# Scores times values on half the rows of the array: two 64-token products with a PSUM bank each, in place of one 128-token product

## The chip, the cores and the metric

The kernel runs on one core of one Trainium2 chip. The metric is the device time of one execution in microseconds (us); the time before is the median of three runs. The engines are named as in the profile: PE is TensorE's matrix multiplication, PEld its loading of the stationary operand, DVE the vector engine, ACT the scalar engine, POOL GpSimd, SP the engine that issues most of the DMAs.

## What is computed

Two layers over one sequence of 4096 tokens of width 256, all in fp32. Each layer normalizes the tokens (`xn`), and adds to the stream an attention-like part and a mixture of experts. The change is in the first layer's attention-like part:

```python
CHUNK = 32
Q = x @ W_q.T
K = x @ W_k.T
V = x @ W_v.T
decay = jax.nn.sigmoid(log_decay[0])
pos = jnp.arange(C)                      # C = CHUNK
diff = pos[:, None] - pos[None, :]
mask = jnp.where(diff >= 0, decay ** diff, 0)
...
S = jnp.einsum('bncd,bnkd->bnck', Qc, Kc) * mask
O = jnp.einsum('bnck,bnkd->bncd', S, Vc).reshape(B, T, D)
gate = jax.nn.sigmoid(x @ W_g.T)
out = gate * O @ W_o.T + x
```

A token sees only the tokens of its own chunk of 32, up to itself. Seen over 128 tokens the score matrix is therefore block-diagonal, in blocks of 32, and so also in blocks of 64. The first layer's other part has 16 experts (keys 256x128, values 128x256 each), all of which run for every token. The second layer is a linear scan with four mixtures and eight routed experts; the change does not touch it.

## The kernel before

The first layer runs over eight groups of 512 tokens (`GROUPS` = 8, `GT` = 512), a group being `JT` = 4 tiles of 128 tokens; the width 256 is `DC` = 2 parts of 128. Within a group a loop `for k in range(E0)` goes over the 16 experts. For expert k PE runs `up(k + 1)`, six matmuls with 512 moving columns into PSUM bank 0 or 1 (helper `mm3`, L397 to L399), and then `down(k)`, twelve matmuls with 256 moving columns into banks 2 to 5 (L1218 to L1220). ACT makes the rounded half of the hidden tile (`relu_hi`, L896), DVE the remainder (`relu_lo`, L1015), and `down(k)` waits for that remainder. Both engines also take the results of `down` out of PSUM (DVE L1060, ACT L936).

The attention-like part is slipped in between experts, in a fixed order written out by hand. It shares banks 6 and 7 (`side2 = ps[:, 6:8, :]`), whose use is passed on through the semaphores `side_full` (PE has written) and `side_free` (ACT or DVE has read).

- After `down(4)` PE makes the scores (L1281): for each tile, each of the two parts of the width and each half h of 64 tokens, one matmul with all 128 rows of the array and 64 of its columns. Half 0 uses columns 0 to 63 of the array, half 1 columns 64 to 127. The halves alternate. DVE masks them into `s32` (L1081), only the two 64x64 diagonal blocks of each tile; the rest of `s32` was set to zero once (`trim_mask`).
- After `down(7)` PE multiplies scores and values (L1289): for each part c of the width and each tile j one fp32 matmul, 128 tokens on 128 rows, 128 columns stationary (`v32`), 128 columns moving (`s32`). Each fp32 matmul shows in the trace as two matmul records with a load each, so eight matmuls show as sixteen. The last one signals `side_full`.
- DVE then multiplies the result with the gate into `sig_g` (L1093, one instruction over 128x1024) and signals `o_gate`; two transposes (L1097) stand behind it in DVE's order. ACT waits for `o_gate` and makes `oT_h` (L954), and only then `relu_hi` of expert 9; DVE's `relu_lo(9)` follows that, and PE's `down(9)` waits for it.
- DVE makes `oT_l` (L1101) behind that. PE needs both after `down(11)` for the output projection (L1236 to L1238).

All engines run the groups from the same `body(g, first, last)`: group 0, a hardware loop over groups 1 to 5, and groups 6 and 7, so that the product occurs 8 times in an execution. The second layer starts when the first has ended on PE. The lines on which matmuls of both layers lie (L397 to L399) are those of a helper.

Of the kernel before, what the change touches and what calls it, by code (L numbers as in the profile page):

```python
# [27 lines left out]
ALU = mybir.AluOpType  # L28
# [3 lines left out]
P = 128  # L32
# [4 lines left out]
JT = GT // P  # L37
# [12 lines left out]
N_ROUND = (NSLOT + 1) // ROUND  # L50
CHUNK = 32
Q32 = 32
S64 = 64
NL = M + E1
VS = D + E0
# [9 lines left out]
def build(nc, a, out):  # L65
# [13 lines left out]
    def sem(name):  # L79
        return nc.alloc_semaphore(name)  # L80
# [44 lines left out]
    sig_g = ra("sig_g", [P, DC, GT], F32)  # L125
    v32 = ra("v32", [P, JT, D], F32)
    s32 = ra("s32", [P, JT, P], F32)
# [5 lines left out]
    otmp = sig_g[:, 0, :].rearrange("p (j d) -> p j d", j=2)  # L133
    N_Q = P // Q32
    xq = v32[:].rearrange("p j (h k) -> p (j h) k", k=DC * Q32)
    stats0 = ra("stats0", [P, JT, 6], F32)
# [12 lines left out]
    at_post = ra.at  # L149
    gw = ra("gw", [P, DC, P // Q32, Q32], F32R)  # L150
    gw_raw = ra("gw_raw", [P, DC, Q32], F32)
    lgT = ra("lgT", [P, JT, Q32], F32)
    lg_rows = ra("lg_rows", [P, JT, Q32], F32)
    stats1 = ra("stats1", [P, JT, 6], F32)
# [96 lines left out]
    ps = nc.alloc_psum_tensor("ps", [P, 8, 512], F32)  # L251
    side2 = ps[:, 6:8, :]
# [95 lines left out]
    o_gate, o_hi, o_23 = sem("o_gate"), sem("o_hi"), sem("o_23")  # L348
# [23 lines left out]
    def use(g, name, first=False):  # L372

        start = 2 if first else 8 * g + 1
        return start + USES.index(name)
# [92 lines left out]
    def chunk_of(rows, j, c):  # L468

        return rows[:, j, c:D:DC]  # L470
# [71 lines left out]
    def mixture_transpose(pe, mx, part, bank):  # L542
        pe.wait_ge(r_comb, part)
        return pe.transpose(ps[0:mixture_rows(mx), bank, 0:P], mx["comb"][:].rearrange("p t m -> p (t m)"), ident[:])
# [155 lines left out]
    with nc.Block("all") as block:  # L700
# [285 lines left out]
        def _(dve):  # L986
# [47 lines left out]
            def body(g, first, last):  # L1034
# [12 lines left out]
                for k in range(E0):  # L1047
# [27 lines left out]
                    if k == 4:  # L1075
# [3 lines left out]
                        for h, done in ((0, mask_s_near), (1, side_free)):  # L1079
                            t = slice(h * S64, (h + 1) * S64)  # L1080
                            dve.tensor_tensor(s32[t, :, t], ps[t, 6, 0:JT * S64].rearrange("p (j c) -> p j c", j=JT),  # L1081
                                              maskT[t, t].unsqueeze(1).to_broadcast((S64, JT, S64)),
                                              ALU.mult).then_inc(done, 1)
                    if k in (10, 11) and not first:
                        c = k - 10
# [4 lines left out]
                        gate_logits(dve, g - 1)  # L1090
                    if k == 7:
                        dve.wait_ge(side_full, use(g, "o", first) + 1)
                        dve.tensor_tensor(sig_g[:], side2, sig_g[:], ALU.mult).then_inc(o_gate, 1)  # L1093
                    if k == 7 and not first:
                        dve.wait_ge(nq_in, 16 * N_Q * g)
                        for c in range(DC):
# [1 line left out]
                    if k in (8, 9):  # L1098
                        c = k - 8
# [30 lines left out]
                    if k == 5 and first:  # L1130
                        dve.wait_ge(gw_ready, 1)
                        gate = gw_raw[:, :, 0:NL].unsqueeze(2).to_broadcast((P, DC, P // Q32, NL))
# [24 lines left out]
            with dve.Fori(1, GROUPS - 2) as g:  # L1157
                body(g, False, False)
            body(GROUPS - 2, False, False)
            body(GROUPS - 1, False, True)  # L1160

        @block.tensor
        def _(pe):
            def body(g, first, last):
                def ready(name):
                    pe.wait_ge(side_free, freed(g, name, first))

                def weights(name):
                    if first:
                        pe.wait_ge(w_lo, chunks[name][0] + 1)  # L1170

                def up(k):

                    if first and k == 0:
                        pe.wait_ge(k0_lo, 1)
                    else:
                        weights(f"keys{k // 4}")
                    if not (first and k < 2):
                        pe.wait_ge(h_lo, E0 * g + k - 1)
                    s = slice(k * H0, (k + 1) * H0)  # L1180
                    for c in range(DC):
                        if k == 0:
                            if first:
                                pe.wait_ge(side_hi, 1 + c)
                            else:
                                pe.wait_ge(xT_hi_ok, DC * (g - 1) + c + 1)
                            pe.matmul(ps[:, 0, :], keys_h[:, c, s], xT_h[:, c, :], start=c == 0, stop=False)
                            pe.matmul(ps[:, 0, :], keys_l[:, c, s], xT_h[:, c, :], start=False, stop=False)
                            continue
                        last = mm3(pe, ps[:, k % 2, :], keys_h[:, c, s], keys_l[:, c, s], xT_h[:, c, :], xT_l[:, c, :],  # L1190
                                   c == 0, c == DC - 1)
                    if k == 0:
                        for c in range(DC):
                            if first:
                                pe.wait_ge(side_free, 1 + c)
                            else:
                                pe.wait_ge(xT_lo_ok, DC * (g - 1) + c + 1)
                            last = pe.matmul(ps[:, 0, :], keys_h[:, c, s], xT_l[:, c, :], start=False, stop=c == DC - 1)
                    last.then_inc(h_full, 1)
# [23 lines left out]
                def project(n):  # L1223
                    weights(n)
                    for o in range(DC):
                        for c in range(DC):
                            s = slice(o * P, (o + 1) * P)
                            last_mm = mm3(pe, side2[:, o, :], PW[n][0][:, c, s], PW[n][1][:, c, s], xT_h[:, c, :],
                                          xT_l[:, c, :], c == 0, c == DC - 1)
                    last_mm.then_inc(side_full, 1)  # L1230
# [20 lines left out]
                if first:  # L1251
                    pe.wait_ge(w_in[chunks["qk"][0] % N_STAGE], 16)
                    for j in range(DC):
                        for o in range(DC):
                            last_mm = pe.matmul(wqk_ps[:, j, :], wqk_raw[:, 0, o, j * P:(j + 1) * P], wqk_raw[:, 1, o, :],
                                                start=o == 0, stop=o == DC - 1)
# [4 lines left out]
                for k in range(E0):  # L1261
                    if 1 <= k < E0 - 1:
                        up(k + 1)
                    if first and k == 1:
                        weights("qk")
                    down(k)
                    if k == 1:
                        ready("v23")
                        project("qk")
                    if k == 2:  # L1270
                        ready("q")
                        project("g")
                    if k == 4:
                        ready("g")
                        if first:
                            pe.wait_ge(xT_sum, 1)
                        for j in range(JT):
                            for c in range(DC):
                                for h in range(P // S64):
                                    t = slice(j * P + h * S64, j * P + (h + 1) * S64)  # L1280
                                    last_mm = pe.matmul(ps[h * S64:(h + 1) * S64, 6, j * S64:(j + 1) * S64], xT[:, c, t],  # L1281
                                                        qT[:, c, t], start=c == 0, stop=c == DC - 1)
                        last_mm.then_inc(side_full, 1)
                    if k == 7:
                        pe.wait_ge(mask_s_near, 3 + g + 1)
                        ready("s")
                        for c in range(DC):
                            for j in range(JT):
                                last_mm = pe.matmul(side2[:, c, j * P:(j + 1) * P], v32[:, j, c * P:(c + 1) * P],  # L1289
                                                    s32[:, j, :], start=True, stop=True)  # L1290
                        last_mm.then_inc(side_full, 1)
                    if k == O_STEP:
                        pe.wait_ge(oT_near, g + 1)
                        ready("o")
                        weights("o")
                        for j in range(JT):
                            last_mm = rows_times(side4[:, j, :], oT_h, oT_l, j, *PW["o"])
                        last_mm.then_inc(side_full, 1)
                    if k == E0 - 4:
                        pe.wait_ge(o_23, g + 1)  # L1300
                        pe.wait_ge(acc01, N01 * g + 2 * (O_STEP + 1) + 1)
                        if not first:
                            post_logits(pe, g - 1)
                    if k == E0 - 3 and last:
                        mixture_transpose(pe, mix1, 1, 7).then_inc(mix_full, 1)
# [9 lines left out]
            for c in range(DC):  # L1315
                for j in range(JT):
                    if c == 0:
                        pe.wait_ge(xn0, j + 1)
                    last_mm = pe.transpose(side2[:, c, j * P:(j + 1) * P], chunk_of(xn, j, c), ident[:])
# [975 lines left out]
```

## Time and profile before

| what | value |
|---|---|
| three runs, median (lowest to highest) | 1006.68 us (1006.67 to 1007.61) |
| the profiled execution's own time | 1007.34 us |
| its span, from first to last instruction | 1005.6 us |
| PE busy in the span | 998.7 us |
| PEld busy | 898.6 us |
| DVE busy | 795.8 us |
| ACT busy | 630.7 us |
| POOL busy | 395.4 us |
| granted clock of TensorE, mean | 1.000 of full |

The profiled execution took 1007.34 us, of which 1.7 us lie outside the span of instructions, and 0.66 us more than the median of the runs. Busy times overlap between engines. The matmuls are pipelined: the time of one matmul in the trace runs from its start to a modelled end, well after the next has started, so what a stream of matmuls costs is read from the distance between starts, not from the duration of one.

### The profile page before, as it was taken

How to read it: one execution, taken by the hardware profiler on the slowest of the kernel's cores; microseconds unless marked ns; L12 is line 12 of the kernel's file. 1: busy time of each engine (PE TensorE's matmuls, PEld its weight loads, DVE VectorE, ACT ScalarE, POOL GpSimd, SP SyncE). 2: the span in 40 equal slices, each digit the busy share in tenths (PEclk: the TensorE clock that was granted, in tenths of full speed). 3: DMA queues.
4: the chain of work that ended last, by engine and by line, in shares of the span. 5: the costliest groups of instructions: out<-in, count | busy, mean ns of one | idle time of the engine just before them, and what ended most of it. 6: DMA issues, size and time to landing. Idle time of an engine off the chain costs nothing.

```text
span 1005.6 us, 20373 instructions
## 1 busy us (share of the span) xinstructions
PE 998.7 (99%) x6494; PEld 898.6 (89%) x6494; DVE 795.8 (79%) x1343; ACT 630.7 (63%) x1219; POOL 395.4 (39%) x393
## 2 busy tenths in 40 slices
PE   8999999999999999999999999999999999999998
PEld 7898989989899898998888888999999999888887
DVE  6876867768686687979789898987788787688897
ACT  4553545545455364554666666988898988566665
POOL 3443444444444444433563864122222220266400
PEclk9999999999999999999999999999999999999999
DMA  6227313122132231452374366688888887645913
GB/s 188 77 71 239 103 45 83 42 83 83 42 83 83 63 104 43 123 213 64 135 301 174 125 234 229 193 289 291 259 271 277 283 261 241 224 135 135 203 43 42
DMA packets 121123, 155.31 MB, mean 154 GB/s; under 512 B 49200, under 2 KB 89136, under 8 KB 120048
## 3 DMA queue, kind: packets, MB, share of 16 engines
q1 hardware_dynamic: 100912, 133.42, 40.6%
q0 software_dynamic: 14464, 15.61, 7.0%
q10 hardware_dynamic: 5696, 5.64, 1.7%
q8 instruction: 27, 0.44, 0.2%
q14 instruction: 24, 0.20, 0.1%
HBM read 110.26 MB, written 44.37 MB: 154 GB/s over the span
## 4 chain that ended last, share of the span: by engine, by line
PE 98%; DMA 1%; DVE 0%; SPq 0%; ACT 0%; DVEq 0%; issue 0%
PE ps L397 19%; PE ps L399 19%; PE ps L398 19%; PE ps L1218 6%; PE ps L1219 6%; PE ps L1220 6%; PE ps L1634 4%; PE ps L1635 4%; PE ps L1636 4%; PE ps L1618 2%; PE ps L1237 2%; PE ps L1236 2%; PE ps L1238 2%; PE ps L1289 1%; PE ps L1281 1%; DMA stage<-wv 1%
## 5 line engine op out<-in xcount | busy, mean ns | idle before, releaser
L845 POOL TENSOR_TENSOR acc<-acc,ytmp 128x512 f32<-128x512 f32 x120 | 158.0, 1317 | 238.5 <-ACT ytmp L936 218.7
L1674 ACT ACTIVATE act_o<-ps,scan_bias 128x512 f32<-128x512 f32 x189 | 129.7, 689 | 92.0 <-PE ps L399 86.9
L936 ACT ACTIVATE ytmp<-ps,sel 128x256 f32<-128x256 f32 x256 | 107.5, 472 | 87.8 <-PE ps L1220 87.0
L1015 DVE SCALAR_TENSOR_TENSOR hT_l<-ps,hT_h 128x512 fp32r<-128x512 f32 (+1 forms) x136 | 88.4, 655 | 80.3 <-ACT hT_h L896 80.1
L1218 PE MATMUL ps<-vals_h,hT_h 128*128 128x256 f32 x512 | 144.4, 282 | 0.0
L1219 PE MATMUL ps<-vals_l,hT_h 128*128 128x256 f32 x512 | 143.7, 281 | 0.0
L1220 PE MATMUL ps<-vals_h,hT_l 128*128 128x256 f32 x512 | 143.4, 280 | 0.0
L896 ACT ACTIVATE hT_h<-ps 128x512 fp32r<-128x512 f32 x128 | 76.5, 597 | 86.3 <-PE ps L399 80.6
L1871 POOL DMA_DIRECT2D rows<-xs_d x92 | 52.9, 577 | 169.0 <-DVE sT L2122 154.1
L1060 DVE SCALAR_TENSOR_TENSOR acc<-ps,sel,acc 128x256 f32<-128x256 f32 x240 | 104.0, 474 | 3.0 <-PE ps L1220 2.8
L1218 PEld LDWEIGHTS ps<-vals_h,hT_h 128*128 128x128 f32 x512 | 96.3, 188 | 6.0 <-issue 0.9
L2046 DVE TENSOR_TENSOR_SCAN h_b<-a_b,hstate,xs_b 128x512 f32<-128x512 f32 x63 | 81.8, 1299 | 23.8 <-ACT a_b L1681 17.9
L1219 PEld LDWEIGHTS ps<-vals_l,hT_h 128*128 128x128 f32 x512 | 96.2, 188 | 4.6
L1220 PEld LDWEIGHTS ps<-vals_h,hT_l 128*128 128x128 f32 x512 | 97.0, 190 | 0.0
L397 PE MATMUL ps<-xT_h,keys_h 128*128 128x512 f32 x240 | 96.5, 402 | 0.0
L399 PE MATMUL ps<-xT_h,keys_l 128*128 128x512 f32 x240 | 95.0, 396 | 0.0
L398 PE MATMUL ps<-xT_l,keys_h 128*128 128x512 f32 x240 | 94.7, 395 | 0.0
L1634 PE MATMUL ps<-w_h,eT_h 128*128 128x256 f32 x312 | 88.6, 284 | 0.0
L1635 PE MATMUL ps<-w_l,eT_h 128*128 128x256 f32 x312 | 88.1, 282 | 0.0
L1636 PE MATMUL ps<-w_h,eT_l 128*128 128x256 f32 x312 | 87.7, 281 | 0.0
L2139 DVE TENSOR_TENSOR eT_l<-t,eT_h 128x512 fp32r<-128x512 f32 (+1 forms) x92 | 55.8, 607 | 30.9 <-ACT eT_h L1720 30.0
L397 PE MATMUL ps<-x1T,WB_late 128*128 128x512 f32 (+2 forms) x198 | 76.9, 389 | 0.0
(261 smaller groups left out, 2792.0 us busy)
## 6 DMA issues: line engine op xcount, KB each, us to landing
raw<-w SPq DMA_DIRECT2D x78, 512.0 KB, 5.4
x1T<-xT_d SPq DMA_DIRECT2D x16, 512.0 KB
comb_b<-comb_d SPq DMA_DIRECT2D x8, 1024.0 KB
w_small<-w SPq DMA_DIRECT2D x16, 512.0 KB, 5.5
xn_d<-xn SPq DMA_DIRECT2D x15, 512.0 KB, 3.0
xs_d<-zeros ACTq DMA_DIRECT2D x1, 4992.0 KB, 19.4
x_d<-x SPq DMA_DIRECT2D x8, 512.0 KB, 4.5
xT_d<-nT_h SPq DMA_DIRECT2D x8, 512.0 KB, 2.7
```

Of the source, the lines that this page charges most:

```text
L397: pe.matmul(dst, wh, xh, start=start, stop=False)
L398: pe.matmul(dst, wh, xl, start=False, stop=False)
L399: return pe.matmul(dst, wl, xh, start=False, stop=stop)
L845: pool.tensor_tensor(dst[:, 2:4, :], acc[:, 2:4, :], ytmp[:, k % 2, :, :], ALU.add).then_inc(acc23, 1)
L936: act.activation(ytmp[:, k % 2, j - 2, :], yb(k, j), ACT.Copy, scale=sel[:, j, k:k + 1]).then_inc(y_23, 1)
L1218: pe.matmul(yb(k, j), hT_h[:, k % 2, s], vals_h[:, k, :], start=True, stop=False)
L1219: pe.matmul(yb(k, j), hT_h[:, k % 2, s], vals_l[:, k, :], start=False, stop=False)
L1220: last_mm = pe.matmul(yb(k, j), hT_l[:, k % 2, s], vals_h[:, k, :], start=False, stop=True)
L1634: pe.matmul(dst, eT_h[:, j, t], w2_h[:, j, :], start=j == 0, stop=False)
L1635: pe.matmul(dst, eT_h[:, j, t], w2_l[:, j, :], start=False, stop=False)
L1636: last_mm = pe.matmul(dst, eT_l[:, j, t], w2_h[:, j, :], start=False, stop=j == FJ - 1)
L1674: act.activation(act_o[:, i % 2, w, :], ps[:, 3 * (i % 2) + w, :], func, bias=scan_bias[:, w, i:i + 1]).then_inc(act_g, 1)
```

## The change

The score product is made by halves of a tile. Each matmul takes 64 tokens on 64 rows of the array and 64 moving columns (128 stationary columns as before). Half 0 uses rows 0 to 63 and writes bank 6, half 1 rows 64 to 127 and bank 7; the halves alternate. There are 16 matmuls a group in place of 8. The blocks of the scores between the halves, which are zero, are no longer multiplied. The result lies in another order in PSUM, by half, so that the gate product on DVE becomes two instructions over 128x512 in place of one over 128x1024, with the signal on the second.

```diff
+S_HALF = 64
...
                         dve.wait_ge(side_full, use(g, "o", first) + 1)
-                        dve.tensor_tensor(sig_g[:], side2, sig_g[:], ALU.mult).then_inc(o_gate, 1)
+                        for h in (0, 1):
+                            t = slice(h * S_HALF, (h + 1) * S_HALF)
+                            gate = sig_g[:].rearrange("p c (j t) -> p (c j) t", j=JT)[:, :, t]
+                            mixed = ps[:, 6 + h, :].rearrange("p (q t) -> p q t", t=S_HALF)
+                            gated = dve.tensor_tensor(gate, mixed, gate, ALU.mult)
+                        gated.then_inc(o_gate, 1)
...
                         ready("s")
                         for c in range(DC):
                             for j in range(JT):
-                                last_mm = pe.matmul(side2[:, c, j * P:(j + 1) * P], v32[:, j, c * P:(c + 1) * P],
-                                                    s32[:, j, :], start=True, stop=True)
+                                for h in (0, 1):
+                                    t, at = slice(h * S_HALF, (h + 1) * S_HALF), (c * JT + j) * S_HALF
+                                    last_mm = pe.matmul(ps[:, 6 + h, at:at + S_HALF], v32[t, j, c * P:(c + 1) * P],
+                                                        s32[t, j, t], start=True, stop=True)
                         last_mm.then_inc(side_full, 1)
```

## Rows read from the trace of the kernel before

**Rows 1.** The page: span, busy time by engine, granted clock in 40 slices.
```profile
span 1005.6 us, 20373 instructions
...
PE 998.7 (99%) x6494; PEld 898.6 (89%) x6494; DVE 795.8 (79%) x1343; ACT 630.7 (63%) x1219; POOL 395.4 (39%) x393
...
PEclk9999999999999999999999999999999999999999
```

**Rows 2.** The page: the chain that ended last, by engine.
```profile
PE 98%; DMA 1%; DVE 0%; SPq 0%; ACT 0%; DVEq 0%; issue 0%
```

**Rows 3.** Waits of PE: who was waited for, total us, times, longest; longest row.
```profile
PE ps L1312 <- POOL ident L815: 2.3, 1, 2.3
```

**Rows 4.** Line 1289's instructions: duration in ns, least, median and most.
```profile
L1289 PEld LDWEIGHTS ps<-s,v x128: 187/192/193, 45.9 to 471.5; 128*128 128x128 f32 x128
L1289 PE MATMUL ps<-s,v x128: 272/275/275, 46.0 to 471.6; 128*128 128x128 f32 x128
```

**Rows 5.** Timeline of PE around line 1289: start, us, instructions.
```profile
105.88 0.28 PE L1220 MATMUL ps<-vals_h,hT_l 128*128 128x256 f32 x1
106.00 1.95 PE L1289 MATMUL ps<-s,v 128*128 128x128 f32 x16
107.70 0.48 PE L397 MATMUL ps<-xT_h,keys_h 128*128 128x512 f32 x1
108.03 0.40 PE L398 MATMUL ps<-xT_l,keys_h 128*128 128x512 f32 x1
108.26 0.40 PE L399 MATMUL ps<-xT_h,keys_l 128*128 128x512 f32 x1
```

**Rows 6.** Timeline of PE around line 1281, the scores.
```profile
96.03 0.28 PE L1219 MATMUL ps<-vals_l,hT_h 128*128 128x256 f32 x1
96.15 0.28 PE L1220 MATMUL ps<-vals_h,hT_l 128*128 128x256 f32 x1
96.36 1.15 PE L1281 MATMUL ps<-qT,xT 128*64 128x64 f32 x32
97.44 0.50 PE L397 MATMUL ps<-xT_h,keys_h 128*128 128x512 f32 x1
97.78 0.39 PE L398 MATMUL ps<-xT_l,keys_h 128*128 128x512 f32 x1
```

**Rows 7.** Line 1281's instructions: duration in ns, least, median and most.
```profile
L1281 PEld LDWEIGHTS ps<-qT,xT x256: 133/138/138, 36.3 to 461.1; 128*64 128x64 f32 x128
L1281 PE MATMUL ps<-qT,xT x256: 222/222/270, 36.3 to 461.2; 128*64 128x64 f32 x128
```

**Rows 8.** Line 1592's matmuls, fp32 with 256 moving columns: duration in ns.
```profile
L1592 PE MATMUL ps<-onehot,ones x2: 378/378/379, 536.9 to 537.1; 128*128 128x256 f32 x2
```

**Rows 9.** Line 1281 in two stretches: instructions under way in each, with clock.
```profile
96.60:96.61 0.01, 0.01 (x8) 0.01 (x6) 1.00 0.00 0
96.60:97.19 0.59, 0.59 (x28) 0.59 (x26) 1.00 0.05 14
```

**Rows 10.** Timeline of PEld at the end of line 1281.
```profile
97.44 0.19 PEld L397 LDWEIGHTS ps<-xT_h,keys_h 128*128 128x128 f32 x1
97.55 0.19 PEld L398 LDWEIGHTS ps<-xT_l,keys_h 128*128 128x128 f32 x1
```

**Rows 11.** Timeline of DVE, ACT and PEld from the gate product to `down(9)`.
```profile
107.99 1.22 DVE L1093 TENSOR_TENSOR sig_g<-ps,sig_g 128x1024 f32<-128x1024 f32 x1 [1.10 <-PE ps L1289]
...
109.24 1.06 ACT L954 ACTIVATE oT_h<-sig_g 128x1024 fp32r<-128x1024 f32 x1 [2.13 <-DVE sig_g L1093]
110.21 0.58 ACT L896 ACTIVATE hT_h<-ps 128x512 fp32r<-128x512 f32 x1
...
110.82 0.69 DVE L1015 SCALAR_TENSOR_TENSOR hT_l<-ps,hT_h 128x512 fp32r<-128x512 f32 x1 [0.40 <-ACT hT_h L896]
...
111.80 0.19 PEld L1218 LDWEIGHTS ps<-vals_h,hT_h 128*128 128x128 f32 x1
```

**Rows 12.** A DVE product from PSUM over 128x512: busy us, mean ns, idle before.
```profile
L1120 DVE TENSOR_TENSOR acc<-ps,acc 128x512 f32<-128x512 f32 x8 | 5.5, 692 | 1.4 <-PE ps L1238 1.2
```

## The prediction

> **What bounds the kernel now.** I read the page first: of a span of 1005.6 us PE is busy for 998.7, and the granted clock is at its upper level, 2.4 GHz, in all 40 slices [rows 1]. The chain that ended last is PE's for 98% [rows 2], and among PE's own waits, four rows in all, the longest comes once, before the first tile, and is 2.3 us [rows 3]. So PE waits for nobody in the eight groups of the first layer, and what the change adds to PE's stream or takes from it goes into the total one for one, unless it makes another engine late. The question is therefore how many ns PE spends per product, before and after.
>
> **The product now.** One matmul of L1289 lasts 275 ns in the trace, but sixteen of them take much less than sixteen times that, since they overlap [rows 4, 5]. I measure a block from the start of the last matmul before it to the start of the second one after it, and take off what these two neighbours cost in a stream: 0.12 us for a 256-column matmul (96.03 to 96.15 [rows 6]) and 0.23 us for a 512-column one (108.03 to 108.26 [rows 5]). The second neighbour is needed because the first matmul after a block has a longer record. For L1289: 108.03 - 105.88 = 2.15 us, less 0.35, is 1.80 us, or 0.112 us for each of the 16. What limits them? The matmul of 256 moving columns lasts 378 ns [rows 8], that of 128 lasts 275 [rows 4], that of 64 lasts 222 [rows 7]: 103 ns for 128 columns, 53 ns for 64, so an fp32 column costs 0.8 ns, and 128 of them 0.105 us. The loads are as long: 192 ns for 128 stationary columns, 138 ns for 64 [rows 4, 7], so 54 ns for 64 columns, 0.108 us for 128. Where a load is seen alone, after L1281, the next load starts 0.11 us behind it [rows 10], and the matmul that had to wait for it lasts 0.50 us instead of 0.39 [rows 6]. So today streaming (0.105 and some ns of handover) just covers the loading (0.108).
>
> **What the change does to it.** It halves the moving columns and the rows, and doubles the number of matmuls; it leaves the stationary columns at 128. Per group there will be 32 records: 32 loads of 128 columns and 32 streams of 64. The nearest thing in the trace is L1281, which also has 32 records in two independent tiles of the array, but splits the columns of the array, not the rows. There two matmuls run at once: the count of instructions under way goes from 8 to 28 when the stretch grows by 0.58 us, so 20 start in 0.58 us, two per 0.058 us [rows 9], while one 64-column stream alone is 0.053. The whole block is 97.78 - 96.15 = 1.63, less 0.35, 1.28 us [rows 6]. Sixteen pairs at 0.058 are 0.93, so 0.35 us are the price of splitting the array: the first load starts 0.21 us after the last `down` matmul instead of 0.12, that load and the first one after the block are not hidden, and the array runs empty before L397's load (last matmul at 96.36 + 1.15 - 0.22 = 97.29, load at 97.44) [rows 6, 7, 10].
>
> Now the term that no row shows: a load of 128 columns into 64 rows. From below it could go with the rows, 0.054 us; from above it is a full load, 0.11 us, since halving the columns is the only thing seen to shorten a load [rows 4, 7]. I take the full load, because the change does not halve the columns. And two loads, one in each half, might run side by side or one behind the other; in L1281 they run side by side, since 32 loads of 0.054 would be 1.73 us and the block is 1.28 [rows 6, 7]. I take side by side, as there. Then a pair of matmuls costs 0.11 us in place of 0.058, for the load hides the stream of 0.053 beneath it. Block: L1281's 1.28 us, plus 15 pairs times (0.11 - 0.058) = 0.78, plus 0.05 for the longer first load, is 2.11 us, against 1.80. That is 0.31 us more per group, 2.5 us over 8 groups. With 0.10 for the pair it is 1.96 and 1.3 us in all, with 0.112 it is 2.14 and 2.7 us. Without any price for the split it is 16 x 0.11 = 1.76, 0.3 us less than before in all.
>
> The section on LDWEIGHTS of the Trainium skill's page "TensorE: Matmul & The Clock Gate" says that the time of a load goes by the number of columns and not by the rows in use, about columns/1.2 ns: 107 ns here. The trace agrees for full rows, 54 ns for each 64 columns [rows 4, 7], and shows nothing for half of them; by this rule alone the pair is 0.107 us and the block 2.07 us.
>
> **The DVE part.** One instruction of 1.22 us [rows 11] becomes two over 128x512; a product of that size with a PSUM operand takes 0.69 [rows 12], so 1.38, 0.16 us more, 1.3 us of DVE in all. It lies beside PE's work. Behind it hangs a chain: `sig_g` until 109.21, ACT's `oT_h` to 110.30, `hT_h` of expert 9 to 110.79, DVE's `hT_l` from 110.82 to 111.51, and PE's first load of `down(9)` at 111.80 [rows 11]. There is 0.29 us of slack, and PE itself gets later against the last product's end by the split's idle stretch, which adds to it. 0.16 fits in. I cost it at nothing. `s32`, its zeroed corners and the two banks' hand-over stay as they are: one signal, one wait. No DMA changes.
>
> **The rivals.**
> (A) My forecast: pairs side by side, each as long as a full load, with the price of the split. +1.3 to +2.7 us, taken +2.5. Chance 0.60.
> (B) A load into 64 rows takes half as long, or two of them as long as half a full one each. Then the pair is 0.058 as in L1281, the block 1.28, and 0.52 us per group are gained: -4.2 us, 1002.5. For it speaks that L1281 shows a pair in that time at all; against it that L1281 halves the columns. It decides from the point where the block is 1.80: 1.33 + 15 x (pair - 0.058) = 1.80, a pair of 0.089 us. Chance 0.12. This is also what the section "Theoretical Speedup" of the Trainium skill's page "TensorEngine Tiling (Array Packing)" promises for a contraction of 64 or less, up to 2 times.
> (C) The array takes only one load at a time when the rows are split. 32 loads of 0.11: the 16 further ones add 16 x 0.11 = 1.76 to 2.11, so 3.87, 2.07 per group, +16.6 us, 1023.3. For it speaks that no row shows two loads in different rows; against it that L1281's go side by side. Chance 0.10.
> (D) Loading and streaming don't overlap within a half: a pair is 0.11 + 0.053, 0.163, the block 1.33 + 15 x 0.105 = 2.91, +8.9 us, 1015.6. In L1281 they do overlap (0.058, not 0.107). Chance 0.06.
> (E) Splitting by rows costs no draining, and the loads are hidden from the first on: 1.76 to 1.80, -0.3 to 0 us, 1006.5. Only splitting by columns is seen to cost something [rows 6]. Chance 0.10.
> (F) DVE's two instructions each cost what the one did, 1.22: `sig_g` comes 1.22 later, 0.29 is slack, PE waits 0.9 us a group in `down(9)`, +7.4 us over A, about 1016.6. L1120's 692 ns speak against it [rows 12]. Chance 0.02.
>
> **How the numbers follow.** The sum is made in the profiled execution: 1007.34 us, of which 1005.6 are the span; +2.5 gives 1009.8 there. That execution lies 0.66 above the median of 1006.68, and I forecast the median: 1006.68 + 2.5 = 1009.2 us. Bounds: A, E and B together hold 0.82, from B's 1002.5 to A's 1009.4, with some tenths for the spread of the runs: 1002.3 to 1010.2. A's own range is 1008.0 to 1009.6. A measurement of this kernel tells about 0.2%, 2.0 us, from no change; A's lower end lies under that. So slower holds most of A (0.52), C, D and F: 0.70. Within 0.2% are the rest of A (0.08) and E: 0.18. Faster is B: 0.12.
>
> **What would show it.** In the changed kernel's profile: 256 loads and 256 matmuls on the product's line, the matmul at about 222 ns, the load at about 190 ns (B: 138). In a stretch of 0.55 us inside the block 10 matmuls start (A), 20 (B), 5 (C), 7 (D). The block by my measure 2.1 us, with the first load 0.2 us after the last `down` matmul and L397's record at about 0.50 us. DVE has 16 products of about 690 ns, and PE still has no wait for `hT_l`. I am wrong if the load's length goes with the rows, if loads in the two halves queue behind each other, or if the price of the split is another one for rows than for columns.

## The result: slower by 0.2%, and the profile after

The changed kernel takes 1009.21 us (median of 11 runs, 1008.87 to 1010.1), the kernel before, run beside it, 1007.28 us (11 runs, 1006.6 to 1007.61). The medians are 1.9 us apart. The ratio of the runs is 1.0023, with a 95% interval of 1.0015 to 1.0031: 1.5 to 3.1 us more, 2.3 in the middle. It was forecast at 1009.2, 2.5 above the median of the three runs shown then. In the profiled executions the span goes from 1005.6 to 1008.1 us.

The page after, the rows that answer to [rows 1, 2]:

```profile
span 1008.1 us, 20637 instructions
...
PE 1001.0 (99%) x6622; PEld 898.8 (89%) x6622; DVE 797.4 (79%) x1351; ACT 631.0 (63%) x1219; POOL 394.2 (39%) x393
...
PE 99%; DMA 1%; DVE 0%; ACT 0%; DVEq 0%; issue 0%; SPq 0%
```

PE has 128 more matmuls and 2.3 us more of busy time, DVE 1.6 us, of which the gate products, 0.07 us longer in each group, account for 0.6. The chain is PE's as before. Lines have moved: the product is L1297 (was L1289), `down` L1224 to L1226, the six matmuls of `up` L398 to L400, the gate product L1098.

Timeline of PE around the product in group 1 of the changed kernel (start, us), which answers to [rows 5], and of PEld at its end, which answers to [rows 10]:

```profile
105.70 0.28 PE L1226 MATMUL ps<-vals_h,hT_l 128*128 128x256 f32 x1
105.91 2.00 PE L1297 MATMUL ps<-s,v 64*128 64x64 f32 x32
107.84 0.50 PE L398 MATMUL ps<-xT_h,keys_h 128*128 128x512 f32 x1
108.18 0.40 PE L399 MATMUL ps<-xT_l,keys_h 128*128 128x512 f32 x1
```

```profile
107.84 0.19 PEld L398 LDWEIGHTS ps<-xT_h,keys_h 128*128 128x128 f32 x1
107.95 0.19 PEld L399 LDWEIGHTS ps<-xT_l,keys_h 128*128 128x128 f32 x1
```

By the prediction's measure the block is 108.18 - 105.70 - 0.35 = 2.13 us against 1.80 before; the same reading of the other seven groups gives 2.13 or 2.14. The signs of the split are those of the scores' block [rows 6, 10]: the first record 0.21 us behind the last `down` matmul, and a first matmul after it with 0.50 us.

Two stretches of the product, with the instructions under way in each (answers to [rows 9]), and the durations of its instructions (answers to [rows 4]):

```profile
106.15:106.16 0.01, 0.01 (x4) 0.01 (x4) 1.00 1.15 410
106.15:107.14 0.99, 0.99 (x22) 0.99 (x21) 1.00 0.88 302
```

```profile
L1297 PEld LDWEIGHTS ps<-s,v x256: 182/188/188, 45.8 to 473.5; 64*128 64x128 f32 x128
L1297 PE MATMUL ps<-s,v x256: 272/272/320, 45.8 to 473.5; 64*128 64x64 f32 x128
```

From 4 to 22: 18 matmuls start in 0.98 us, two per 0.11 us. The load lasts 188 ns on 64 rows, where it was 192 on 128: it does not go with the rows.

DVE and ACT behind the product, group 1, which answers to [rows 11]:

```profile
107.96 1.29 DVE L1098 TENSOR_TENSOR sig_g<-ps,sig_g 128x512 f32<-128x512 f32 x2 [1.26 <-PE ps L1297]
...
109.28 1.06 ACT L955 ACTIVATE oT_h<-sig_g 128x1024 fp32r<-128x1024 f32 x1 [2.35 <-DVE sig_g L1098]
110.25 0.58 ACT L897 ACTIVATE hT_h<-ps 128x512 fp32r<-128x512 f32 x1
...
110.86 0.69 DVE L1016 SCALAR_TENSOR_TENSOR hT_l<-ps,hT_h 128x512 fp32r<-128x512 f32 x1 [0.40 <-ACT hT_h L897]
```

The two gate instructions take 1.29 us together, 0.07 more than the one. `hT_l` of expert 9 is ready at 111.55, and the load that waits for it comes at 111.95, so 0.40 us of slack are left, more than the 0.29 before: PE got later by more than the chain.

### The profile page after: what moved, and what is told of

Same layout as the page of the kernel before. It is cut to its first block, busy times and chain, and to the rows that moved or that the text cites. A ratio compares the mean times of both kernels' runs of the same rounds, so it can differ in the third digit from the quotient of the medians.

```text
span 1008.1 us, 20637 instructions
## 1 busy us (share of the span) xinstructions
PE 1001.0 (99%) x6622; PEld 898.8 (89%) x6622; DVE 797.4 (79%) x1351; ACT 631.0 (63%) x1219; POOL 394.2 (39%) x393
## 4 chain that ended last, share of the span: by engine, by line
PE 99%; DMA 1%; DVE 0%; ACT 0%; DVEq 0%; issue 0%; SPq 0%
PE ps L398 19%; PE ps L400 19%; PE ps L399 19%; PE ps L1224 6%; PE ps L1225 6%; PE ps L1226 6%; PE ps L1642 4%; PE ps L1643 4%; PE ps L1644 4%; PE ps L1626 2%; PE ps L1243 2%; PE ps L1242 2%; PE ps L1244 2%; PE ps L1297 2%; PE ps L1287 1%; DMA stage<-keys 1%
## 5 line engine op out<-in xcount | busy, mean ns | idle before, releaser
L1224 PE MATMUL ps<-vals_h,hT_h 128*128 128x256 f32 x512 | 144.3, 282 | 0.0
L1226 PE MATMUL ps<-vals_h,hT_l 128*128 128x256 f32 x512 | 143.4, 280 | 0.0
L1224 PEld LDWEIGHTS ps<-vals_h,hT_h 128*128 128x128 f32 x512 | 96.3, 188 | 5.7 <-issue 0.5
L1226 PEld LDWEIGHTS ps<-vals_h,hT_l 128*128 128x128 f32 x512 | 97.1, 190 | 0.0
L398 PE MATMUL ps<-xT_h,keys_h 128*128 128x512 f32 x240 | 96.7, 403 | 0.0
L400 PE MATMUL ps<-xT_h,keys_l 128*128 128x512 f32 x240 | 94.9, 396 | 0.0
L398 PE MATMUL ps<-x1T,WB_late 128*128 128x512 f32 (+2 forms) x198 | 77.0, 389 | 0.0
```

The source lines that it names most:

```text
L398: pe.matmul(dst, wh, xh, start=start, stop=False)
L400: return pe.matmul(dst, wl, xh, start=False, stop=stop)
L1224: pe.matmul(yb(k, j), hT_h[:, k % 2, s], vals_h[:, k, :], start=True, stop=False)
L1226: last_mm = pe.matmul(yb(k, j), hT_l[:, k % 2, s], vals_h[:, k, :], start=False, stop=True)
```

## The experiments

Theory L says that the pair costs 0.112 us because two loads of 128 stationary columns run side by side and hide the streams of 64. Its rival S says that a stream on half the rows is itself slow. What made S worth a test is that the product's matmul lasts 272 ns, not the 222 that I had forecast for 64 moving columns. All blocks below are read as above, in group 1. The first four kernels were run once each, and the kernel before beside them took 1006.79 us; within each of the four traces the block has the same length in all eight groups, to 0.01 us, but for three groups of the fourth kernel (see the last section).

**Fewer stationary columns** (a quarter of the product is left out).

```diff
-last_mm = pe.matmul(ps[:, 6 + h, at:at + S_HALF], v32[t, j, c * P:(c + 1) * P],
+last_mm = pe.matmul(ps[0:96, 6 + h, at:at + S_HALF], v32[t, j, c * P:c * P + 96],
                     s32[t, j, t], start=True, stop=True)
```

> The changed kernel with 96 instead of 128 stationary columns in each product matmul (64 rows and 64 moving columns as there); a quarter of the product is left out. Theory L, the load of the stationary columns sets the time of a pair: 0.084 us a pair instead of 0.112, the block 1.68 us instead of 2.13, the execution 3.6 us shorter than the changed kernel. Theory S, a 64-column stream on half the rows is itself slow (its record is 272 ns, that of a 64-column stream on all rows 222): the pair stays at 0.112, the block at 2.13 us, the time as the changed kernel's.

Timeline of PE, and the durations of its instructions:

```profile
105.72 0.28 PE L1226 MATMUL ps<-vals_h,hT_l 128*128 128x256 f32 x1
105.93 1.57 PE L1297 MATMUL ps<-s,v 64*96 64x64 f32 x32
107.43 0.50 PE L398 MATMUL ps<-xT_h,keys_h 128*128 128x512 f32 x1
107.77 0.40 PE L399 MATMUL ps<-xT_l,keys_h 128*128 128x512 f32 x1
```

```profile
L1297 PEld LDWEIGHTS ps<-s,v x256: 156/162/163, 45.9 to 470.6; 64*96 64x96 f32 x128
L1297 PE MATMUL ps<-s,v x256: 244/245/294, 45.9 to 470.6; 64*96 64x64 f32 x128
```

The block is 1.70 us. The load is 26 ns shorter and the matmul 27, though it streams the same 64 columns: the matmul's record holds a wait for its own load. S falls. The one execution takes 1006.75 us, 2.5 below the changed kernel's median where 8 x 0.43 = 3.4 are missing from the blocks. By the starts of PE's matmuls, 0.36 us of that is lost again in group 0, at the wait of `down(9)` that is told below; the rest cannot be told from the spread, since single executions of the kernel before lie up to 2.0 us apart (1006.75 to 1008.77).

**More moving columns** (part 1 of the width is written over part 0).

```diff
-t, at = slice(h * S_HALF, (h + 1) * S_HALF), (c * JT + j) * S_HALF
-last_mm = pe.matmul(ps[:, 6 + h, at:at + S_HALF], v32[t, j, c * P:(c + 1) * P], s32[t, j, t], ...)
+t, at = slice(h * S_HALF, (h + 1) * S_HALF), j * P
+last_mm = pe.matmul(ps[:, 6 + h, at:at + P], v32[t, j, c * P:(c + 1) * P], s32[t, j, :], ...)
```

> The changed kernel with 128 instead of 64 moving columns in each product matmul, part 1 of the width written over part 0, so that the product is not complete. Theory L: the pair stays at 0.112 us, since a stream of 128 columns is just as long as a load, the block is 2.13 to 2.18 us and the time that of the changed kernel within 0.5 us. Theory S: the pair grows with the stream to 0.16 to 0.22 us, the block to 2.9 to 3.8, the execution 6 to 13 us above the changed kernel.

```profile
105.71 0.28 PE L1226 MATMUL ps<-vals_h,hT_l 128*128 128x256 f32 x1
105.92 2.06 PE L1297 MATMUL ps<-s,v 64*128 64x128 f32 x32
107.90 0.50 PE L398 MATMUL ps<-xT_h,keys_h 128*128 128x512 f32 x1
108.24 0.40 PE L399 MATMUL ps<-xT_l,keys_h 128*128 128x512 f32 x1
```

Twice the stream, and the block is 2.18 us: 0.05 more, which is the last pair's longer stream, that no load covers. The one execution takes 1009.9 us. The change's saving in moving columns was worth nothing, because they lay under the loads.

**All rows, no split.**

```diff
-... v32[t, j, c * P:(c + 1) * P], s32[t, j, t], ...
+... v32[:, j, c * P:(c + 1) * P], s32[:, j, t], ...
```

> The changed kernel with all 128 rows in each product matmul (the other half's scores are zero), still 64 moving columns: no splitting of the array. Theory L: 32 loads one behind the other, 0.112 us each, the block 3.6 us, the first load as early as before, some 14 us above the kernel before. Theory S: 32 streams of 0.058 us, the block 1.9 us, some 1 us above the kernel before.

```profile
107.36 0.28 PE L1226 MATMUL ps<-vals_h,hT_l 128*128 128x256 f32 x1
107.48 3.68 PE L1297 MATMUL ps<-s,v 128*128 128x64 f32 x32
110.97 0.48 PE L398 MATMUL ps<-xT_h,keys_h 128*128 128x512 f32 x1
111.29 0.39 PE L399 MATMUL ps<-xT_l,keys_h 128*128 128x512 f32 x1
```

The block is 3.58 us, 0.112 for each of 32 loads one behind the other, and the first matmul starts 0.12 us after the last `down` one: no price of a split. 1021.02 us, 14.2 above the kernel before, where 8 x 1.78 = 14.2 were to come. So the split itself earns something, two loads at once; the change spends it on having twice as many loads, and pays the 0.35 us on top.

**The halves not alternating.**

```diff
-for c in range(DC):
-    for j in range(JT):
-        for h in (0, 1):
-            t, at = slice(h * S_HALF, (h + 1) * S_HALF), (c * JT + j) * S_HALF
+for h in (0, 1):
+    t = slice(h * S_HALF, (h + 1) * S_HALF)
+    for c in range(DC):
+        for j in range(JT):
+            at = (c * JT + j) * S_HALF
```

> The changed kernel with the same 16 matmuls a group in another order: first all of half 0, then all of half 1. If the halves run side by side only where they alternate in the program: 32 records of 0.112 us one behind the other and the price of the split, 3.9 us a block, some 17 us above the kernel before. If the array pairs them whatever the order: 2.13 us a block, as the changed kernel.

Timeline of PE, and the line's matmuls and loads under way in four stretches, two in half 0 and two at the passage to half 1:

```profile
106.95 0.28 PE L1226 MATMUL ps<-vals_h,hT_l 128*128 128x256 f32 x1
107.16 3.39 PE L1298 MATMUL ps<-s,v 64*128 64x64 f32 x32
110.48 0.50 PE L398 MATMUL ps<-xT_h,keys_h 128*128 128x512 f32 x1
110.82 0.39 PE L399 MATMUL ps<-xT_l,keys_h 128*128 128x512 f32 x1
```

```profile
107.60:107.61 0.01, 0.01 (x2) 0.01 (x2) 1.00 0.59 205
107.60:108.05 0.45, 0.45 (x6) 0.45 (x5) 1.00 0.95 330
108.55:108.56 0.01, 0.01 (x4) 0.01 (x3) 1.00 0.00 0
108.55:108.98 0.43, 0.43 (x10) 0.43 (x9) 1.00 0.04 5
```

The block is 3.52 us, where I had expected 3.9 or 2.13. Within half 0 four matmuls start in 0.44 us, one per 0.11; at the passage six in 0.42. The missing 0.4 us are some four records of half 0 beside which half 1 was already begun. So the two halves run side by side only where their matmuls stand near each other in the program, and the alternation keeps them there; this run differs from the changed kernel in nothing else. Theory C of the prediction is excluded by the changed kernel; this run shows what it would have looked like: 1024.78 us. Of the 18 us, 8 x 1.72 = 13.8 are the blocks. The rest goes with the clock, as the last section shows.

**The product in quarters of the array.** The load is what counts, so it is halved too: 64 stationary columns, four tiles of 64x64.

```diff
-pe.wait_ge(mask_s_near, 3 + g + 1)
-ready("s")
+wait_alone(pe, mask_s_near, 3 + g + 1)
+wait_alone(pe, side_free, freed(g, "s", first))
...
-last_mm = pe.matmul(ps[:, 6 + h, at:at + S_HALF], v32[t, j, c * P:(c + 1) * P],
-                    s32[t, j, t], start=True, stop=True)
+for q in (0, 1):
+    r, o = slice(q * 64, (q + 1) * 64), c * P + q * 64
+    last_mm = pe.matmul(ps[r, 6 + h, at:at + S_HALF], v32[t, j, o:o + 64],
+                        s32[t, j, t], start=True, stop=True)
```

PE's two waits ahead of the block become instructions of their own. The first matmul still starts 0.21 us behind the last `down` one, as in the changed kernel, so they cost nothing that shows.

> The product in quarters of the array: 64 tokens on 64 rows and 64 stationary columns, so that four matmuls in four tiles of the array run at once (two halves of the tokens, two halves of the width part), 32 matmuls a group; PE waits in two instructions of its own ahead of the block. Theory L: a load is now 64 columns, four side by side, 0.058 us for each four, the block 1.28 us as the scores' block, 0.5 us less than before, 4.1 us less in all, 0.4% faster than the kernel before. Theory S: four matmuls in 0.112 us, the block 2.1 us, as the changed kernel. Third possibility, the four records are handed out no faster than two per 0.058 us: the block 2.2 us, 0.3% slower than before.

Timeline of PE, two stretches inside the block, and the load's duration:

```profile
105.82 0.28 PE L1226 MATMUL ps<-vals_h,hT_l 128*128 128x256 f32 x1
106.03 1.16 PE L1299 MATMUL ps<-s,v 64*64 64x64 f32 x64
107.12 0.50 PE L398 MATMUL ps<-xT_h,keys_h 128*128 128x512 f32 x1
107.46 0.39 PE L399 MATMUL ps<-xT_l,keys_h 128*128 128x512 f32 x1
```

```profile
106.30:106.31 0.01, 0.01 (x15) 0.01 (x9) 1.00 0.29 102
106.30:106.88 0.58, 0.58 (x54) 0.58 (x48) 1.00 1.05 360
```

```profile
L1299 PEld LDWEIGHTS ps<-s,v x512: 129/135/135, 46.0 to 467.6; 64*64 64x64 f32 x171
```

39 matmuls start in 0.57 us, four per 0.058, the load is 135 ns, and the block 1.29 us. The execution takes 1003.52 us (5 runs, 1003.33 to 1003.63) against 1007.0 before (15 runs), a ratio of 0.9963, 0.9949 to 0.9977. It is faster than both kernels.

**The gate product in two on DVE, alone**, in the kernel before.

```diff
-dve.tensor_tensor(sig_g[:], side2, sig_g[:], ALU.mult).then_inc(o_gate, 1)
+for c in range(DC):
+    gated = dve.tensor_tensor(sig_g[:, c, :], side2[:, c, :], sig_g[:, c, :], ALU.mult)
+gated.then_inc(o_gate, 1)
```

> The kernel before with only the gate product on DVE in two instructions of 128x512, the signal on the second. If the DVE part is hidden, as I costed it: within 0.3 us of the kernel before, 0.16 us more of DVE per group, no wait of PE for hT_l. If it is not hidden: up to 1.3 us more.

1007.01 us (11 runs) against 1007.0 (15 runs), ratio 0.9999, 0.999 to 1.0008. The two instructions are cut by the parts of the width and not by the halves of the tokens, but they last 681 ns each, as the changed kernel's 682. DVE's part is hidden, within what can be measured. All of the change's cost is PE's.

**Where the quarters' missing gain went.** Eight blocks shorter by 0.51 us are 4.0 to 4.1 us, the median went down by 3.5. I compared the starts of PE's matmuls in the two traces: up to `down(9)` of group 0 the kernel in quarters had gained 0.6, and there it lost it again. Timeline of PEld at that place with quarters, and of DVE:

```profile
52.09 0.19 PEld L1224 LDWEIGHTS ps<-vals_h,hT_h 128*128 128x128 f32 x1 [0.95 <-issue]
```

```profile
45.94 1.20 DVE L1003 TENSOR_TENSOR keys_l<-stage,keys_h 128x1024 fp32r<-128x1024 f32 x1
...
48.44 1.28 DVE L1098 TENSOR_TENSOR sig_g<-ps,sig_g 128x512 f32<-128x512 f32 x2
...
51.33 0.69 DVE L1016 SCALAR_TENSOR_TENSOR hT_l<-ps,hT_h 128x512 fp32r<-128x512 f32 x1 [0.97 <-ACT hT_h L897]
```

DVE's `hT_l` of expert 9 ends at 52.02 and the load follows at 52.09. In group 0 DVE also splits the weights (L1003), so the gate product starts late, at 48.44, 1.36 us behind the first matmul after the product (47.08), where in group 1 of the same kernel it is 0.13; and ACT makes `hT_h` only behind `oT_h`. This chain did not get shorter with the product. The next two kernels put `oT_h` behind `hT_h` of expert 9, once with the quarters, once in the kernel before.

```diff
 if 1 <= k < E0 - 1:
     relu_hi(g, k + 1, first)
+if k == 8:
+    act.wait_ge(o_gate, g + 1)
+    act.activation(oT_h[:], sig_g[:], ACT.Copy).then_inc(o_hi, 1)
...
-if k == 7:
-    act.wait_ge(o_gate, g + 1)
-    act.activation(oT_h[:], sig_g[:], ACT.Copy).then_inc(o_hi, 1)
```

> The product in quarters, and on ACT the making of oT_h moved behind the hT_h of expert 9, so that hT_l of expert 9 no longer hangs on the gate product. If the gain missing from the quarters (4.0 us less in the eight blocks, 3.5 to 3.7 in the execution) was lost to PE's wait for hT_l in group 0, that wait of 0.7 us goes and the execution is 0.5 to 0.7 us shorter than with quarters alone, 4.1 us shorter than the kernel before. If it was lost elsewhere, the time is that of quarters alone.

> The kernel before with ACT's two instructions in that other order alone. The wait of PE in group 0 is 0.2 us there and goes; the other groups had slack: 0.2 us shorter, not to be told from no change. A rival: oT_h is now late for the output projection, and PE waits there in every group: slower.

With the quarters: 1002.2 us (5 runs, 1002.07 to 1003.08) against 1006.93 (14 runs), ratio 0.9951, 0.9937 to 0.9965. Timeline of PE in group 0, at the same `down(9)`:

```profile
50.70 0.39 PE L400 MATMUL ps<-xT_h,keys_l 128*128 128x512 f32 x1
50.93 0.28 PE L1224 MATMUL ps<-vals_h,hT_h 128*128 128x256 f32 x1
```

PE goes on 0.23 us after the last `up` matmul: the wait is gone. By the starts of PE's matmuls in the two traces the new order is worth 0.8 us at this place, a little more than I had expected, and another 0.17 at `down(11)` of the same group, where PE had a short wait too. The medians differ by 1.3, but each was measured beside other runs of the kernel before and the intervals of the two ratios overlap, so no more is claimed than the trace shows. In the kernel before, the trace has both waits gone as well, 0.2 and 0.17 us, and no new one at the output projection, which was the rival. The time is 1007.1 us (11 runs) against 1006.93, ratio 0.9999, 0.999 to 1.0008: not to be told from no change, as expected.

## Why the prediction was right, point by point

The first point rests on these lines of the kernel before, the timelines of PE and of PEld at `down(9)` of group 0:

```profile
51.77 0.40 PE L399 MATMUL ps<-xT_h,keys_l 128*128 128x512 f32 x1
52.14 0.36 PE L1218 MATMUL ps<-vals_h,hT_h 128*128 128x256 f32 x1
```

```profile
52.11 0.19 PEld L1218 LDWEIGHTS ps<-vals_h,hT_h 128*128 128x128 f32 x1 [0.38 <-issue]
```

- **PE's stream decides, one for one**: right, with one flaw. The eight blocks are 8 x 0.333 = 2.7 us longer, and the span 2.5. But "PE waits for nobody in the eight groups" was wrong for group 0. There the first matmul of `down(9)` started 0.37 us after the last of `up`, instead of 0.23, and lasted 0.36 instead of 0.28, which together is a wait of 0.2 us for the chain of [rows 11]. The list of PE's waits did not show it, since it stood as 0.38 us of "issue" of PEld. In the changed kernel the later product hides it, and takes 0.2 us off the cost. That makes 2.5 us. A second wait, 0.17 us at `down(11)` of group 0, is in both traces and changes nothing here. Besides, the changed kernel's trace has its first experts 0.3 us earlier and the second layer 0.4 us longer, which about cancels; neither was followed up.
- **A load of 128 columns into 64 rows is a full load**: right. 188 ns against 192 [rows 4], and the cost follows the stationary columns when they alone are changed (96 columns: block 1.70; 128: 2.13) and not the moving ones (128 in place of 64: 2.18). The rule of the Trainium skill's page "TensorE: Matmul & The Clock Gate", section on LDWEIGHTS, holds here for half the rows too.
- **The two halves' loads run side by side**: right, two matmuls per 0.11 us. Kept apart in the program they don't, except for the last few.
- **The price of the split, 0.35 us**: right. 2.13 - 16 x 0.112 = 0.34; without the split it is 3.58 - 32 x 0.112 = 0.0.
- **The sum**: 0.31 us a group forecast, 0.33 measured; the pair was nearer to 0.112 than to 0.11. That this agrees is no luck, since the pair and the price of the split were each measured. That the forecast median of 1009.2 was met to 0.01 us is luck: the kernel before came out at 1007.28 this time, 0.6 above the 1006.68 that the sum started from, and the medians are 1.9 us apart and not 2.5. (The upper end of A is given once as 1009.4 and once as 1009.6; its own terms, 1006.68 + 2.7, give 1009.4.)
- **DVE hidden**: right; 0.07 us more instead of 0.16, and with that alone no difference in time.
- **A sign that I got wrong**: I forecast a matmul of 222 ns and it was 272. I had read the step from 222 [rows 7] to 275 [rows 4] as streaming. But with 64 moving columns on all rows, where loads limit, the matmul lasts 275 as well: the record takes in the wait for its own load. That the stream of 64 columns costs about 0.053 us follows from the 103 ns between 128 and 256 columns, and the longer last stream of 0.05 us, and the sum didn't change.
- **The rivals**: B, the gain of 4 us, fails with the load on half the rows, yet its size is what the quarters reach once the stationary columns are halved too (block 1.29, forecast for B 1.28). C and D are out by two per 0.11 us, E by the 0.34 us, F by 1.29 us for both gate instructions. The speedup of up to 2 times for a short contraction, in the section "Theoretical Speedup" of the Trainium skill's page "TensorEngine Tiling (Array Packing)", does not come here: the block went from 1.80 to 2.13 us, since the array was waiting for loads.

## What to carry to other kernels

Before splitting a small matmul over half the rows of the array, count the loads. In fp32 a load of stationary columns took about as long here as a stream of as many moving ones (0.11 us for 128, 0.05 for 64), on 64 rows as on 128, so that a 128x128 product is on the edge already, and halving rows and moving columns only doubles the loads. Halve the stationary columns as well, let the tiles alternate in the program, and weigh the gain against the fixed price of the split, here 0.35 us per block by columns, 0.34 by rows and 1.29 - 16 x 0.058 = 0.36 in quarters. And when PE gets faster at one place, look for the wait that was just short of showing: it sat in the first group, where other engines had more to do.

## What the runs showed of the hardware that I had not expected

With the halves kept apart, the granted clock fell three times, each time at the end of a block, in three of the eight groups (3, 5 and 7, counted from 0). Three stretches of PE in group 3 (start:end, busy and matmuls, clock), and two of its matmuls behind the block:

```profile
231.70:234.70 3.00, 3.00 (x32) 1.00 0.46 158
235.20:238.20 3.00, 3.00 (x9) 0.50 0.48 108
238.70:241.70 3.00, 3.00 (x22) 1.00 0.20 28
```

```profile
235.80 0.63 PE L399 MATMUL ps<-xT_l,keys_h 128*128 128x512 f32 x1
236.23 0.63 PE L400 MATMUL ps<-xT_h,keys_l 128*128 128x512 f32 x1
```

The first stretch lies in the block (231.88 to 235.27), where most of the time one half of the array works and waits for its loads. The clock is then at 0.50, 1.2 GHz, and back at 2.4 GHz behind it. In between, matmuls with 512 moving columns start 0.43 us apart, where it is 0.23 at the upper clock. By the starts of PE's matmuls against those of the changed kernel, this cost 1.4, 1.5 and 1.5 us in the three groups, 4.4 in all, and 18.0 - 13.8 = 4.2 were to be explained. The first slowed matmuls also lengthen the block by the measure used here, to 3.78, 3.69 and 3.67 us in these groups, where it is 3.52 in the other five. PE was busy in all three stretches. Neither the changed kernel nor the unsplit one with 3.58 us a block shows such a fall (mean clock 1.000 in both). Only the coincidence is shown, and in one execution: what in the block the fall goes with, half the rows or the gaps between the streams, and why three groups and not eight, stays open. Also new to me: tiles in four quarters are handed out at four per 0.058 us, with no sign of a limit.
